# A transformer block with a routed expert layer on one core: the second norm of the first two sequences placed elsewhere in the order of the steps

## The chip, the cores and the metric

The kernel runs on 1 core of one Trainium2 chip. The metric is the device time of one execution in microseconds (us). Profiles are of one execution each.

## What is computed

Four sequences (b = 0 to 3) of 1024 tokens, width 256, pass through one block:

```python
mod = silu(c) @ wmod                     # sa, ca, ga, sb, cb, gb, per sequence
h = layernorm(x) * (1 + ca) + sa
x = x + ga * attention(h)                # 16 heads of width 16, causal
h = layernorm(x) * (1 + cb) + sb         # "the second norm"
logits = h @ gate_w                      # 8 experts, the best 2 with softmax weights
x = x + gb * sum_of_two_experts(h)       # per expert: silu(h @ w1) @ w2
```

## The kernel before

The kernel is written by hand for five engines: PE (matmuls), ACT (exps, copies, scaling), DVE (maxima, statistics, small arithmetic), POOL (element-wise work on pairs of tiles, and some transfers) and SP (the queue that issues most transfers). Each engine runs its own instructions strictly in order; semaphores tie them together.

`schedule()` writes one list, `order`, of steps. Each engine's program walks through the whole list and issues its own share of every step, so a step's place in the list sets its place on all five engines at once. A wait inside a step holds back everything that stands behind it on that engine, transfers on SP and POOL included.

**The attention** is sixteen groups, four heads each, four groups to a sequence: sequence b is in groups 4b to 4b + 3. This text counts groups from 0, as the code does, so the sixth, seventh, eighth and ninth group are groups 5, 6, 7 and 8. A group has 24 slots. In slot k of group w PE makes two score tiles (`score`, L1738, for the masked ones also L1742, into `PS`), ACT takes their exps (L1091, `PR<-PS`), PE multiplies the exps by V (`pv`, L1758). The other half of a slot belongs to a later group: two tiles for the row maxima (`max`, L1715 on PE into `PM`, L1425 and L1428 on DVE), 34 slots ahead (`LEAD`). So the maxima of group w + 2 begin in slot 14 of group w. There are three `PM` banks and three `PS` banks, so PE is held when DVE or ACT fall behind by more than that.

`place(w, k, parts)` puts a chain of steps into group w at slot k; each part has a delay in slots from the part ahead of it. Around the groups these chains run, and the change touches or meets them:

- `rep(g)`, group g - 2, slot 2, on SP: 12 transfers `QK<-SD` (L724) and a small one `QK<-ZR` (L758) that bring group g's split queries and keys on chip. PE's first `max` of group g waits for all of them. Every second group `sd` is ahead of it (slot 23 of an odd group, six stores `SD<-SP`, L737).
- `od(g - 1)`, group g, slot 4, on POOL: five small transfers (L708 `OP<-OS`, L709 `LD<-OS`) of a group's results and row sums.
- `lsum`, `recip`, `lrec`, `lrep` for a pair of groups, in groups 2, 4, 6, ... from slot 7: SP reads the row sums back (`LP<-LD`, L806), DVE takes their reciprocal at slot 11 (L1460, it waits for that transfer), SP writes them out (L809) and reads them spread (L814, `LP<-LR`); POOL's `div` at slot 17 (L954) uses them. `out(b)`, group 4b + 4 from slot 20, makes the attention's output on PE (L1770) and adds it on POOL (L960, L965).
- The second norm of sequence b: `x2` (SP stores x, L818), `stat2` (DVE, 8 tiles, bn_stats and bn_aggr, L1336 and L1338), `rstd` (16 small dependent DVE instructions on 128x8, L1364 to L1383, a root by Newton steps; the code calls turn 2 for this norm), `h2` (four pairs of tiles: two ACT instructions each, L1119, then two POOL instructions, L984 and L987), `h2st` (SP waits for all four `h2` and stores h, L823, `H2D<-XA`, 1 MB).
- The router's logits of sequence b, four times `lgt` (PE transposes, L1779; ACT copies, L1124), `lg` (PE, L1787; DVE copies, L1469), `top` (DVE, L1476 and L1478).

For b = 0 and 1 the helper `ln2(b)` is one chain from slot 10 of group 4b + 7: store and eight statistics, one per slot, sixteen root steps at half slots, `h2` three slots later and one per slot, then `h2st`; it runs into slots 5 to 9 of group 4b + 8, where the logits stand at slots 9, 11, 13 and 15.

After the groups come the routed experts (L1625 on PE) and the sum of the outputs; the change moves nothing there.

Of the kernel before, what the change touches and what calls it, by code (L numbers as in the profile page):

```python
# [16 lines left out]
NT = T // 128  # L17
# [91 lines left out]
def schedule():  # L109
# [10 lines left out]
    def place(w, k, parts):  # L120
        at.setdefault(NW * w + k, []).append(parts)
# [18 lines left out]
    def ln2(b, wait=3, pace=1, rest=0.5, n4=4):  # L140
        parts, d = [(0, ("x2", b))], 0
        for n in range(NT):
            parts.append((d, ("stat2", b, n)))
            d = 1 if n % pace == pace - 1 else 0
        parts += [(d if n == 0 else rest if n % (n4 if pace > 1 else 1) == 0 else 0, ("rstd", 2, b, n, 2)) for n in range(16)]
        return parts + [(1 if tp else wait, ("h2", b, tp)) for tp in range(4)] + [(1, ("h2st", b))]
# [4 lines left out]
    def logits(b, tp, rest=0.5):  # L151
        return [(0, ("lgt", b, tp)), (1, ("lg", b, tp)), (rest, ("top", b, tp, 0)), (rest, ("top", b, tp, 1))]
# [16 lines left out]
    def one(*step):  # L169
        return [(0, step)]  # L170
# [35 lines left out]
        for tp, k in enumerate((20, 22, 23, 25)):  # L206
            place(4 * b + 4, k, one("out", b, tp))
    for b in range(B - 2):
        place(4 * b + 7, 10, ln2(b))
        for tp in range(4):  # L210
            place(4 * b + 8, 9 + 2 * tp, logits(b, tp))
    place(NG - 3, 4, ln2(B - 2, 2, 2))
    for tp in range(4):
        place(NG - 3, 16 + 2 * tp, logits(B - 2, tp))
# [230 lines left out]
def adaln_block(nc, x, wqkvT, b_qk, b_v, woT, b_o, gate_w, w1, w2, cT, wmod, iota, out):  # L445
# [8 lines left out]
    with ctx:  # L454
# [140 lines left out]
        LR = nc.dram_tensor("LR", [2 * B, 8, T], F32).ap()  # L595

        order = schedule()
        names = dict.fromkeys(n for by in (FIRST, *SIGNALS.values()) for n in by)
        S = {n: Signal(ctx.enter_context(nc.semaphore(f"s_{n}"))) for n in names}
# [1308 lines left out]
```

## Time and profile before

| | us |
|---|---|
| median of 3 runs | 981.04 (980.57 to 982.25) |
| the profiled execution | 978.13 |
| its span in the profile | 976.4 |
| PE busy in the span | 881.6 (90%) |
| DVE busy | 704.4 (72%) |
| ACT busy | 579.8 (59%) |
| POOL busy | 387.5 (40%) |
| granted PE clock, mean | 0.983 |

The span is the time from the first to the last profiled instruction; some 1.7 us of the execution lie outside it. Busy time is the time in which an engine executes; a matmul's end is modelled, so a busy PE need not be at its peak. The profile's clock column is the share of the full 2.4 GHz that PE was granted.

### The profile page before, as it was taken

Reading aid. Unit: us, or ns where it says so; the run is one execution under the profiler, and the core shown is the slowest. Engines: PE = TensorE matmul, PEld = TensorE weight load, DVE = VectorE, ACT = ScalarE, POOL = GpSimd, SP = SyncE. Lnnn points to the kernel's source line nnn. Section 1 sums busy time; section 2 is a strip of 40 time slices with the busy share of each in tenths; the row PEclk is TensorE's granted clock in tenths of the full one; section 3 lists DMA queues with packets and bytes.
Section 4 is the critical chain, followed back from the end, with each engine's and each line's share of the span. In section 5 each row is a group of like instructions: output and inputs, shape, how many; then the busy total and the mean of one; then the engine's idle time right before and its main releaser. Section 6 shows DMA issues by size and latency. Waiting matters only on the chain.

```text
span 976.4 us, 19311 instructions
## 1 busy us (share of the span) xinstructions
PE 881.6 (90%) x6091; PEld 527.3 (54%) x6164; DVE 704.4 (72%) x2285; ACT 579.8 (59%) x1268; POOL 387.5 (40%) x386
## 2 busy tenths in 40 slices
PE   7898899998999998999999987878899999999990
PEld 3453444433535434544443443432799899999980
DVE  7887777879566889657689667899547575444588
ACT  3365477676676777586676757767535433333563
POOL 4213101731531435333143554124586465555630
PEclk8999999999999999999999999999999999999995
DMA  5487436525506437244364663206332323222699
GB/s 204 125 177 173 61 87 99 83 82 89 80 2 145 76 72 161 67 64 107 64 123 103 131 129 131 74 26 180 111 97 77 98 77 103 77 77 75 207 297 317
DMA packets 83596, 110.62 MB, mean 113 GB/s; under 512 B 16290, under 2 KB 56794, under 8 KB 83498
## 3 DMA queue, kind: packets, MB, share of 16 engines
q1 hardware_dynamic: 73194, 84.22, 36.3%
q0 software_dynamic: 9216, 22.80, 9.1%
q10 hardware_dynamic: 1088, 2.36, 0.7%
q8 instruction: 53, 0.87, 0.4%
q14 instruction: 45, 0.37, 0.1%
HBM read 69.42 MB, written 35.41 MB: 107 GB/s over the span
## 4 chain that ended last, share of the span: by engine, by line
PE 59%; DVE 11%; ACT 5%; DMA 4%; issue 4%; POOL 1%; SPq 1%; DVEq 0%; ACTq 0%; POOLq 0%
PE PY L1625 10%; PE PH L1625 10%; PE PO L1758 9%; PE PS L1738 8%; PE PM L1715 6%; PE PHT L1843 3%; ACT PR L1091 3%; PE PX L1770 3%; DVE MXF L1428 2%; DMA LD<-OS 2%; DVE JK L1425 2%; PE PX L1694 2%; PE PX L1690 2%; PE PS L1742 2%; PE PX L1679 1%
## 5 line engine op out<-in xcount | busy, mean ns | idle before, releaser
L1091 ACT ACTIVATE PR<-PS 128x512 f32<-128x512 f32 (+3 forms) x768 | 334.5, 498 | 126.5 <-PE PS L1742 92.6
L1425 DVE CUSTOM_DVE_ANT_0 JK<-PM,MK 128x128 bf16<-128x128 f32 (+3 forms) x512 | 238.4, 483 | 51.2 <-PE PM L1715 48.4
L1715 PE MATMUL PM<-QK 128*128 128x512 bf16 (+3 forms) x725 | 230.5, 326 | 27.0 <-DVE MXF L1428 12.7
L1738 PE MATMUL PS<-QK 128*128 128x512 bf16 (+3 forms) x738 | 233.4, 328 | 11.4 <-ACT PR L1091 9.1
L1428 DVE TENSOR_REDUCE MXF<-PM 128x1 f32<-128x512 f32 x256 | 175.0, 684 | 78.0 <-PE PM L1715 61.4
L1738 PEld LDWEIGHTS PS<-QK 128*128 128x128 bf16 x768 | 75.0, 98 | 165.9 <-ACT PR L1091 106.4
L1758 PE MATMUL PO<-PR,V 128*17 128x512 f32 (+3 forms) x1536 | 161.0, 491 | 0.0
L1715 PEld LDWEIGHTS PM<-QK 128*128 128x128 bf16 x768 | 75.0, 98 | 99.9 <-DVE MXF L1428 33.4
L1625 PE MATMUL PY<-W2S,HT 128*128 x852 | 119.3, 289 | 2.7 <-issue 1.8
L1742 PE MATMUL PS<-MT,identb 128*128 128x128 bf16 x512 | 111.4, 220 | 2.7 <-DMA QK<-CD 1.4
L1625 PE MATMUL PH<-W1S,XT 128*128 x426 | 111.7, 397 | 0.6 <-DVE W2S L1580 0.6
L1154 ACT ACTIVATE HS<-PH 128x512 f32<-128x512 f32 x71 | 42.4, 597 | 114.6 <-PE PH L1625 114.6
L1625 PEld LDWEIGHTS PY<-W2S,HT 128*128 128x128 f32 x852 | 106.4, 190 | 3.2 <-issue 3.2
L1015 POOL DMA_INDIRECT YT<-YO,ROW x71 | 75.4, 1062 | 75.3 <-DVE YO L1600 43.5
L1588 DVE TENSOR_TENSOR XT<-PXT,XT 128x256 fp32r<-128x256 f32 x71 | 29.9, 422 | 98.0 <-ACT XT L1148 97.7
L1009 POOL DMA_INDIRECT XL<-H2D,TOK x71 | 78.4, 1105 | 46.2 <-PE PXT L1822 20.6
L1625 PEld LDWEIGHTS PH<-W1S,XT 128*128 128x128 f32 x426 | 75.7, 189 | 13.4 <-issue 0.8
L932 POOL TENSOR_TENSOR SF<-SF,SP 128x512 f32<-128x512 f32 x28 | 32.6, 1163 | 126.0 <-ACT SP L1081 124.7
L708 POOL DMA_DIRECT2D OP<-OS x60 | 29.7, 501 | 112.8 <-ACT OS L1098 112.4
L1742 PEld LDWEIGHTS PS<-MT,identb 128*128 128x128 bf16 x512 | 50.4, 98 | 29.8 <-issue 3.2
L954 POOL TENSOR_TENSOR OP<-OP,LP 128x1024 f32<-128x1024 f32 x7 | 16.5, 2355 | 100.9 <-DMA LP<-LR 78.6
L1593 DVE TENSOR_TENSOR HT<-PHT,HT 128x512 fp32r<-128x512 f32 x71 | 49.0, 690 | 3.9 <-ACT HT L1162 0.2
(284 smaller groups left out, 1199.4 us busy)
## 6 DMA issues: line engine op xcount, KB each, us to landing
QK<-SD SPq DMA_DIRECT2D x180, 128.0 KB
SD<-SP SPq DMA_DIRECT2D x42, 256.0 KB, 3.0
LP<-LR SPq DMA_DIRECT2D x64, 64.0 KB
W1S<-in_w SPq DMA_DIRECT2D x8, 512.0 KB, 7.2
OP<-OS POOLq DMA_DIRECT2D x60, 64.0 KB, 6.5
X<-XA SPq DMA_DIRECT2D x3, 1024.0 KB, 11.8
H2D<-XA SPq DMA_DIRECT2D x3, 1024.0 KB, 4.5
YG<-YT SPq DMA_DIRECT2D x12, 256.0 KB, 5.0
```

The lines of the kernel that those rows point to most:

```text
L1009: eng.indirect_dma_start(XL[:, t % 3, :], None, H2D[0:(B if t >= NA else B - 1) * T, :], bass.IndirectOffsetOnAxis(ap=TOK[:, t:t + 1], axi ...
L1015: eng.indirect_dma_start(YT, bass.IndirectOffsetOnAxis(ap=ROW[:, t:t + 1], axis=0), YO[:, t % 4, :], None, bounds_check=EMPTY - 1 + B * T ...
L1091: eng.activation(PR[:, slot, i, c0:512], PS[m % 3][:, c0:512], ACT.Exp, scale=0.25).then_inc(S["exp"].sem, 1)
L1154: eng.activation(HS[:, t % 2, :], PH[t % 2][:, :], ACT.Silu).then_inc(S["silu"].sem, 1)
L1425: eng.tensor_tensor_reduce(JK[:, jk % 2, 0:w], PM[m % 3][:, 0:w], MK[:, 512 - w:512], 1.0, -3.0e38, ALU.add, ALU.max, MXA[:, mb, h, qt:qt ...
L1428: eng.tensor_reduce(MXF[:, mb, h, qt - 4:qt - 3], PM[m % 3][:, 0:w], AX.X, ALU.max).then_inc(S["mx"].sem, 1)
L1593: eng.tensor_tensor(HT[:, t % 2, 1, :, :], PHT[t % 2][:, :, :], HT[:, t % 2, 0, :, :].bitcast(F32), ALU.subtract).then_inc(S["hlo"].sem, 1)
L1625: last = eng.matmul(out_, stat[:, part, c, :], wt[:, bass.ds(v, 1), c, :].rearrange("p a n -> p (a n)"), start=(j == 0 and c == 0), stop=( ...
L1715: eng.matmul(PM[m % 3][:, 0:128 * (k1 - k0)], QK[:, r, h, 0, qt * 128:(qt + 1) * 128], QK[:, r, h, 1, k0 * 128:k1 * 128], start=True, stop ...
L1738: last = eng.matmul(PS[m % 3][:, c0:512], QK[:, r, h, 1, j * 128:(j + 1) * 128], QK[:, r, h, 0, 512 * f + c0:512 * f + 512], start=True, s ...
L1742: last = eng.matmul(PS[m % 3][:, c0:c0 + 128], identb[:, :], MT[:, :], start=False, stop=True, skip_group_check=True)
L1758: last = eng.matmul(PO[32 * i:32 * i + 17, c0:512], V[g // 4 % 2][:, j, 4 * (g % 4) + i, :], PR[:, (m - 1 + i // 2) % SLOTS, i % 2, c0:512 ...
```

## The change

The four steps of the second norm of sequences 0 and 1 are taken apart and placed one by one. `x2` and `stat2` go to slots 6 to 13 of group 4b + 5 (groups 5 and 9), the root steps to group 4b + 6 from slot 4 (groups 6 and 10), the scaling `h2` to slots 19 to 22 of group 4b + 7 (groups 7 and 11), `h2st` to slot 0 of group 4b + 8 (groups 8 and 12). The logits of sequence 0 go from group 8 to group 10; those of sequence 1 stay in group 12. The instructions themselves are the same.

```diff
     for b in range(B - 2):
-        place(4 * b + 7, 10, ln2(b))
+        place(4 * b + 5, 6, [(0, ("x2", b))] + [(1, ("stat2", b, n)) for n in range(NT)])
+        place(4 * b + 6, 4, [(0.5 if n else 0, ("rstd", 2, b, n, 2)) for n in range(16)])
         for tp in range(4):
-            place(4 * b + 8, 9 + 2 * tp, logits(b, tp))
+            place(4 * b + 7, 19 + tp, one("h2", b, tp))
+            place((10, 12)[b], 9 + 2 * tp, logits(b, tp))
+        place(4 * b + 8, 0, one("h2st", b))
```

The changed file is three lines longer, so each line number behind this place is 3 higher in it (L823 is L826, L984 is L987, L1460 is L1463).

SP's queue from the end of group 7 into group 8, before (`SD<-SP` is `sd` of pair 5, `QK<-ZR` and `QK<-SD` are `rep(10)`, `LP` are the row sums of groups 6 and 7, `H2D<-XA` is `h2st`):

```order
70 L737 DMA SD<-SP 128x1024 x6
71 L758 DMA QK<-ZR 3x4x1024
72 L724 DMA QK<-SD 16x4x1024 x12
73 L806 DMA LP<-LD 128x64
74 L823 DMA H2D<-XA 128x8x256
75 L809 DMA LR<-LP 128x64
76 L814 DMA LP<-LR 16x1024 x8
```

and in the changed kernel:

```order
70 L740 DMA SD<-SP 128x1024 x6
71 L826 DMA H2D<-XA 128x8x256
72 L761 DMA QK<-ZR 3x4x1024
73 L727 DMA QK<-SD 16x4x1024 x12
74 L809 DMA LP<-LD 128x64
75 L812 DMA LR<-LP 128x64
76 L817 DMA LP<-LR 16x1024 x8
```

The store of h has moved from behind the row sums to ahead of the 12 copies of `rep(10)`. The same stands at group 12, where `rep(14)` and one weight load come behind it.

POOL at the same place, before (`SF` and `SP` are `qk_hi` and `qk_lo` of pair 5, `OP<-OS` and `LD<-OS` are `od(7)`, `XA<-XA,G` is `h2`):

```order
86 L932 TENSOR_TENSOR SF<-SF,SP 128x512
87 L938 TENSOR_TENSOR SP<-SF,SP 128x512
88 L708 DMA OP<-OS 16x1024 x4
89 L709 DMA LD<-OS 4x1024
90 L984 TENSOR_TENSOR XA<-XA,G 128x512
91 L987 TENSOR_TENSOR XA<-XA,G 128x512
```

and in the changed kernel:

```order
86 L935 TENSOR_TENSOR SF<-SF,SP 128x512
87 L987 TENSOR_TENSOR XA<-XA,G 128x512
88 L990 TENSOR_TENSOR XA<-XA,G 128x512
89 L941 TENSOR_TENSOR SP<-SF,SP 128x512
90 L987 TENSOR_TENSOR XA<-XA,G 128x512
91 L990 TENSOR_TENSOR XA<-XA,G 128x512
92 L987 TENSOR_TENSOR XA<-XA,G 128x512
93 L990 TENSOR_TENSOR XA<-XA,G 128x512
94 L987 TENSOR_TENSOR XA<-XA,G 128x512
95 L990 TENSOR_TENSOR XA<-XA,G 128x512
96 L711 DMA OP<-OS 16x1024 x4
97 L712 DMA LD<-OS 4x1024
```

The eight instructions of `h2` (four pairs) have moved from behind `od(7)` to ahead of it, the first pair also ahead of the last subtraction of `qk_lo`.

## Rows read from the trace of the kernel before

**Rows 1.** Busy us (count) PE, PEld, DVE, ACT, POOL; clock, DMA, GB/s: groups 4, 8, 10, 12
```profile
216.00:254.70 38.70, 34.85 (x248) 15.88 (x250) 32.21 (x123) 23.33 (x53) 9.93 (x10) 1.00 0.46 86
...
369.90:413.80 43.90, 40.29 (x294) 21.72 (x298) 34.99 (x158) 28.64 (x65) 20.11 (x18) 1.00 0.47 90
...
455.80:491.70 35.90, 35.31 (x254) 17.38 (x257) 24.92 (x89) 23.69 (x54) 9.02 (x10) 1.00 0.49 89
...
529.30:571.50 42.20, 40.20 (x295) 21.56 (x299) 28.31 (x127) 28.50 (x66) 20.08 (x18) 1.00 0.56 121
```
**Rows 2.** POOL, groups 7 and 8: start, us, instruction, [idle before <- releaser]
```profile
364.34 1.16 POOL L932 TENSOR_TENSOR SF<-SF,SP 128x512 f32<-128x512 f32 x1
366.22 1.15 POOL L938 TENSOR_TENSOR SP<-SF,SP 128x512 bf16<-128x512 f32 x1 [0.72 <-DVE SP L1401]
374.20 1.96 POOL L708 DMA_DIRECT2D OP<-OS  x4 [6.82 <-ACT OS L1098]
376.15 0.58 POOL L709 DMA_DIRECT2D LD<-OS  x1
377.48 1.26 POOL L984 TENSOR_TENSOR XA<-XA,G 128x512 f32<-128x512 f32 x1 [0.76 <-ACT XA L1119]
...
387.10 1.27 POOL L987 TENSOR_TENSOR XA<-XA,G 128x512 f32<-128x512 f32 x1
399.33 2.35 POOL L954 TENSOR_TENSOR OP<-OP,LP 128x1024 f32<-128x1024 f32 x1 [10.96 <-DVE CP L1449]
```
**Rows 3.** Groups of instructions by line: ACT's half of the scaling
```profile
L1119 ACT ACTIVATE XA<-XA,RT,RS 128x256 f32<-128x256 f32 x24 | 13.1, 600 | 0.0
```
**Rows 4.** SP's issues in order of time, group 8
```profile
370.31 5.58 SPq L724 DMA_DIRECT2D QK<-SD  x12
385.72 0.34 SPq L806 DMA_DIRECT2D LP<-LD  x1
388.47 0.38 SPq L823 DMA_DIRECT2D H2D<-XA  x1
388.90 0.57 SPq L809 DMA_DIRECT2D LR<-LP  x1
393.74 3.57 SPq L814 DMA_DIRECT2D LP<-LR  x8
```
**Rows 5.** Windows of 2 us in group 8, the columns of rows 1
```profile
374.00:376.00 2.00, 2.00 (x17) 0.77 (x17) 2.00 (x8) 1.23 (x4) 1.80 (x4) 1.00 1.12 142
...
384.00:386.00 2.00, 1.84 (x20) 1.42 (x21) 1.67 (x7) 1.39 (x4) 1.78 (x3) 1.00 0.05 9
...
390.00:392.00 2.00, 1.91 (x15) 1.30 (x13) 2.00 (x14) 2.00 (x5) 0.00 (x0) 1.00 1.03 346
```
**Rows 6.** PE in group 8: the first matmul for the maxima of group 10
```profile
390.88 0.22 PE L1715 MATMUL PM<-QK 128*128 128x128 bf16 x1
```
**Rows 7.** DVE in order of time: the reciprocal in groups 4 and 12
```profile
232.76 0.52 DVE L1460 RECIPROCAL LP<-LP 128x64 f32<-128x64 f32 x1
...
548.15 0.55 DVE L1460 RECIPROCAL LP<-LP 128x64 f32<-128x64 f32 x1 [1.55 <-DMA LP<-LD]
```
**Rows 8.** SP's issues in group 12, and the landing of its weight load (last column)
```profile
536.50 0.41 SPq L839 DMA_DIRECT2D W1S<-in_w  x1
545.23 0.34 SPq L806 DMA_DIRECT2D LP<-LD  x1
...
W1S<-in_w SPq DMA_DIRECT2D x1, 512.0 KB, 10.6
```
**Rows 9.** PE and its clock after an early stall: timeline, then windows of 2 us
```profile
46.85 0.22 PE L1722 MATMUL PX<-identb,CPH 128*48 128x128 bf16 x1 [2.15 <-DVE CPH L1449]
...
48.00:50.00 2.00, 1.78 (x6) 0.55 (x5) 2.00 (x7) 0.00 (x0) 1.15 (x1) 0.55 0.03 6
50.00:52.00 2.00, 2.00 (x6) 0.70 (x5) 1.20 (x3) 0.00 (x0) 0.00 (x0) 0.60 0.45 119
```
**Rows 10.** DVE in order of time: a root step of 8 columns in group 8
```profile
399.53 2.17 DVE L1377 TENSOR_TENSOR RT<-RS 128x8 f32<-128x8 f32 x1
```

## The prediction

> **What bounds the kernel now.** I read the busy table of the page first: PE executes in 90% of the span, DVE in 72%. Then the windows by group, whose borders are the first of each group's 48 exps in ACT's timeline. Group 8 lasts 43.9 us with 40.3 of PE, group 12 42.2 with 40.2, group 10 35.9 with 35.3 [rows 1]. So a group costs its PE work plus 0.6 to 3.6 us in which PE stands, and the change can win only out of that, since it removes no instruction. Group 4 (38.7 us, 34.9 of PE) is what group 8 is without logits and scaling: it has the same output steps and the same statistics of a later sequence's first norm. Last, the timelines of POOL and SP, because the change moves work past other work there, and in-order queues make others wait for it.
>
> **What moves and costs nothing.** The eight statistics (groups 5, 9) and sixteen root steps (groups 6, 10) go into groups where DVE has room: in group 10 it is busy 24.9 of 35.9 us [rows 1]. ACT's part of the scaling is eight instructions of 0.60 us [rows 3]; it now stands between the short exps, and POOL needs twice as long for its part, so ACT is no pacer. The store of x goes to group 5, where nobody waits for it. For all four groups together I take +0.6 us (bounds 0 and 2).
>
> **The scaling on POOL.** It now stands behind the fourth subtraction of group 7, which ends at 364.34 + 1.16 = 365.5. The eight instructions took 377.48 to 388.37, or 10.9 us, and one subtraction (1.15, with gaps 1.3) goes in between [rows 2]. So the chain ends at 365.5 + 0.1 + 10.9 + 1.3 = 377.8. Before, POOL was free until 374.20, when it issued the five transfers of group 7's results [rows 2]; these now start 3.6 us later and end about 380.4.
>
> **The store of h on SP.** `h2st` waits for all four pairs, and behind it stand the 12 copies of `rep(10)`. Before, their first was issued at 370.31 [rows 4]; now the store goes at 377.9 and the first copy, behind it and the small copy of zeros, near 379.1: 8.8 us later. The transfers themselves: the store's 1.05 MB moved at 346 GB/s and was through about 4.4 us after its issue at 388.47, since SP's next issue that needed it gone is at 393.74 [rows 4, 5], so it ends at 382.3. The copies with the five transfers beside them are 1.57 + 0.28 MB at 142 GB/s, 13.0 us; before, they were through just after 384 [rows 5]. Now they end at 382.3 + 13.0 = 395.3. PE asked for them at 390.88 [rows 6], and would ask at about 388 with logits and waits gone from the slots ahead. The slack before was 6 us, the delay is 11.
>
> **The row sums.** `LP<-LD` was issued 9.0 us after the last of the five transfers (376.7 to 385.72) [rows 2, 4], so now at about 389.5. But it goes into the same queue as the copies. A small transfer behind a large one lands behind it: `LR<-LP`, 32 KB, was issued at 388.90 right behind the store, and SP could not go on to what needs it before 393.74 [rows 4], just after the store was through. The page "DMA: Bandwidth & Descriptors" of the Trainium skill (Queues, rings and completion order) says that a ring's descriptors are consumed in order; by that rule, the trace agrees, `LP<-LD` waits for the copies; it speaks against this change, and the sum with it is the one below, without it that of rival 1. In group 12 of before the reciprocal came 1.0 us behind the landing of the large load ahead of its row sums (547.1 and 548.15) [rows 7, 8]. So now it starts at 395.3 + 1.0 = 396.3. DVE would reach it 16.8 us after the group's first exp (232.76 - 216.00, group 4) [rows 1, 7], that is near 385 to 387, and behind it stand all later maxima, for which PE waits after three banks. **Both PE's copies and DVE's row sums are late by about 10 us.** From the reciprocal to the next group's first exp it was 254.70 - 232.76 = 21.9 us in group 4 [rows 1, 7]. So group 9 starts at 418.2, against 413.8: **+4.4 us** for group 8, its lost logits already in it.
>
> **Group 12.** POOL's and SP's work repeats 159.5 us later (`LP<-LD` at 545.23 and 385.72) [rows 4, 8]. The chain ends at 537.3, the store is through at 541.8, the copies at 554.8. Behind them is a weight load of 0.52 MB [rows 8], half the store, 1.5 us: 556.3. The reciprocal starts 1.0 later, at 557.3. Before, it started at 548.15, already after 1.55 us of waiting for that transfer [rows 7], which had the weight load (landing 536.50 + 10.6 = 547.1) ahead of it [rows 8]. The logits stay here, so the rest of the group is as it was: **+9.2 us**.
>
> **Logits in group 10.** Group 8 has 40.29 - 34.85 = 5.4 us more PE work than group 4 [rows 1], and I charge them in group 10, with 0.8 us of waits for the shared bank (group 12 stands 2.0 us, group 10 0.6; part of that is scaling): **+6.2** (bounds 5.4 and 7.5).
>
> **The clock.** The groups of before have no stall of PE as long as these. The nearest row: after one of 2.15 us at 46.85, the granted clock was 0.55 and 0.60 in two windows of 2 us [rows 9], so about half, 1.2 of 2.4 GHz, for most of 4 us. While PE is the bound, this costs about 1.7 us. Bounds per stall 0 (the clock holds, or DVE paces) and 3.4 (twice as long); I take 1.7, twice: **+3.4**.
>
> **Sum.** 4.4 + 9.2 + 6.2 + 3.4 + 0.6 = 23.8 us on the profiled 978.13, or 1001.9. The median of the runs is 2.9 above that execution, 981.04, so I forecast 1004.8 for the median after. The gains the change has are in this: the roots beside POOL's work and DVE's full slots in groups 7, 8, 11 and 12 go, but they lie ahead of or inside a stall that a chain on POOL and SP sets, and are swallowed by it.
>
> **Rival 1: only the copies hold.** If `LP<-LD` slips past the copies, it lands near 391.5, and PE is held by its first maximum alone. From that matmul group 8 took 413.8 - 390.9 = 22.9 us, less 2.7 for the two of four logits that follow it: 20.2, so group 9 starts at 415.5, +1.7. In group 12 the same matmul stands at about 529.3 + 21.0 = 550.3 and goes at 554.8: +4.5. With 6.2 + 0.6 and one share of the clock, 1.7, this is +14.7: 995.7. For it: the five transfers use another queue and do get through between the copies. Against: `LP<-LD` doesn't use that queue, and the row of `LR<-LP`. Chance 0.2.
>
> **Rival 2: faster.** The chain on POOL ends early enough, or the copies overtake the store, and nothing is held. Then the waits in the crowded groups go. A root step on 8 columns took 2.17 us [rows 10] beside POOL's product of 2.35 us from 399.33 [rows 2], and the roots of this norm leave such places. The most to win is PE's standing time in groups 8 and 12, 3.6 + 2.0 [rows 1], with 0.8 given back in group 10: 976.2. The page "SBUF — State Buffer" of the Trainium skill (SBUF: two separate sides) has the rule behind it: a DVE instruction with two operands in SBUF and one of GpSimd lock each other out for a whole instruction; by that rule the trace agrees, and the rule is for this change. It decides at the copies: they must be through by about 388, so the store must be gone before 371. The eight instructions at 1.27 us behind 365.5 forbid that; it would need them much shorter or an earlier start, and the order gives neither. Chance 0.07, and 0.03 for gains and stalls that cancel within 0.2% (about what a measurement of this kernel can tell from no change).
>
> **Rival 3: slower still.** Store, copies and POOL's five transfers share the engines worse than in sequence, and the row sums' later legs (`LR`, `LP<-LR`, `div`, `out`) are late too, 3 to 4 us a group, or the clock stays low for twice the time: 1009 to 1015. Chance 0.12. The forecast itself has 0.58.
>
> **Numbers.** The range takes in rival 1 down to its sum without clock and with the lower logits (981 + 1.7 + 4.5 + 5.4 is 992.6, less 1.6 for waits that the statistics' move may end), 991, and part of rival 3, 1012. Faster 0.07, same 0.03, slower 0.90.
>
> **What would show it.** In the trace after: POOL's eight scaling instructions solid from 365.5 to about 378; `H2D<-XA` issued at 378 and `QK<-SD` behind it; DVE idle some 10 us ahead of the reciprocal in group 8 with `LP<-LD` as releaser, 9 in group 12; PE standing as long, and a clock below 1 behind it; group 9 starting 4.4 us later than before, group 10 near 42 us with little standing. I am wrong if the first copy of `rep(10)` goes before 375, if the reciprocal finds its row sums there, or if group 12 is no longer than before.

## The result, and the profile after

| | before | after |
|---|---|---|
| median of the runs, us | 981.38 (980.57 to 982.25, 4 runs) | 1004.46 (1000.04 to 1005.51, 4 runs) |
| ratio, 95% interval | | 1.0231 (1.0209 to 1.0253) |
| the profiled execution, us | 978.13 | 1005.01 |
| its span, us | 976.4 | 1003.3 |
| PE, DVE, ACT, POOL busy, us | 881.6, 704.4, 579.8, 387.5 | 899.3, 700.9, 580.2, 387.6 |
| granted PE clock, mean | 0.983 | 0.963 |

The change costs 23.1 us, 2.3%; the forecast was 1004.8. The two profiled executions lie 26.9 us apart in their spans, because the one of before is faster than its median. The same work is done, so the time lies in stands and in the clock. The windows by group of the changed kernel (columns as in [rows 1]: PE, PEld, DVE, ACT, POOL busy, the granted clock, DMA share, GB/s), for groups 4, 7, 8, 10, 12, 13 and 14:

```profile
214.00:252.50 38.50, 35.09 (x251) 15.95 (x250) 31.91 (x123) 23.20 (x53) 9.93 (x10) 1.00 0.45 86
330.20:366.70 36.50, 35.69 (x242) 14.74 (x240) 26.99 (x92) 28.98 (x66) 15.20 (x17) 1.00 0.45 81
366.70:417.70 51.00, 37.18 (x251) 16.10 (x251) 32.40 (x124) 23.65 (x55) 18.41 (x17) 0.90 0.38 85
459.30:501.00 41.70, 41.39 (x306) 23.16 (x305) 28.36 (x133) 25.99 (x58) 8.97 (x10) 1.00 0.41 78
537.60:593.70 56.10, 44.19 (x300) 23.87 (x300) 28.17 (x120) 25.46 (x59) 18.37 (x17) 0.85 0.39 86
...
593.70:640.40 46.70, 39.92 (x281) 18.37 (x280) 35.12 (x141) 32.11 (x69) 17.73 (x17) 0.93 0.61 160
640.40:679.90 39.50, 31.37 (x283) 13.27 (x281) 34.47 (x118) 24.58 (x56) 6.29 (x10) 0.96 0.13 29
```

Against [rows 1], group 8 went from 43.9 to 51.0 us although it lost the logits, group 12 from 42.2 to 56.1, group 10 from 35.9 to 41.7. In groups 8 and 12 PE is busy 13.8 and 11.9 us less than the window lasts, and the clock is below 1. In group 10 nothing waits: 41.39 of 41.70 is PE work. Groups 7 and 11 are 1.0 us shorter each (36.6 for 37.6 from exp to exp), as the statistics and root steps beside them are gone.

The cause in group 8 is read on three queues. POOL in order of time, against [rows 2]:

```profile
363.49 1.44 POOL L987 TENSOR_TENSOR XA<-XA,G 128x512 f32<-128x512 f32 x1
...
366.43 1.16 POOL L941 TENSOR_TENSOR SP<-SF,SP 128x512 bf16<-128x512 f32 x1
...
374.90 1.27 POOL L990 TENSOR_TENSOR XA<-XA,G 128x512 f32<-128x512 f32 x1
376.11 1.98 POOL L711 DMA_DIRECT2D OP<-OS  x4
403.47 2.35 POOL L957 TENSOR_TENSOR OP<-OP,LP 128x1024 f32<-128x1024 f32 x1 [24.82 <-issue]
```

SP's issues, against [rows 4]:

```profile
376.27 0.37 SPq L826 DMA_DIRECT2D H2D<-XA  x1
...
377.49 9.57 SPq L727 DMA_DIRECT2D QK<-SD  x12
387.17 0.35 SPq L809 DMA_DIRECT2D LP<-LD  x1
394.65 0.34 SPq L812 DMA_DIRECT2D LR<-LP  x1
```

DVE at the stand, in order of time:

```profile
394.07 0.55 DVE L1463 RECIPROCAL LP<-LP 128x64 f32<-128x64 f32 x1 [10.53 <-DMA LP<-LD]
```

and PE:

```profile
395.23 0.61 PE L1718 MATMUL PM<-QK 128*128 128x512 bf16 x1 [10.45 <-DVE MXF L1431]
```

The store of h is issued in the moment in which POOL's last scaling instruction ends (374.90 + 1.27 = 376.17). Behind it the 12 copies need 9.57 us to be issued (5.58 before), the read of the row sums lands 6.9 us after its issue, DVE stands 10.5 us on it, and PE, its three banks full, 10.4 us on DVE. The windows through this stand:

```profile
388.00:390.00 2.00, 0.00 (x0) 0.00 (x0) 0.00 (x0) 0.00 (x0) 0.00 (x0) 0.82 1.06 153
390.00:392.00 2.00, 0.00 (x0) 0.00 (x0) 0.00 (x0) 0.00 (x0) 0.00 (x0) 0.50 1.00 132
392.00:394.00 2.00, 0.00 (x0) 0.00 (x0) 0.00 (x0) 0.00 (x0) 0.00 (x0) 0.50 0.13 23
...
396.00:398.00 2.00, 2.00 (x12) 0.41 (x10) 1.93 (x12) 1.13 (x2) 0.00 (x0) 0.50 0.26 66
```

The DMA engines are full (1.06, 1.00) while every compute engine stands, and idle from 393. The clock falls to half, 1.2 GHz, while PE stands, and is still there when PE works again. Group 12 is the same, later and with the weight load between (SP's issues):

```profile
546.84 0.37 SPq L826 DMA_DIRECT2D H2D<-XA  x1
...
548.06 10.13 SPq L727 DMA_DIRECT2D QK<-SD  x12
558.30 0.40 SPq L842 DMA_DIRECT2D W1S<-in_w  x1
558.80 0.40 SPq L809 DMA_DIRECT2D LP<-LD  x1
```

DVE, and PE behind it:

```profile
566.79 0.55 DVE L1463 RECIPROCAL LP<-LP 128x64 f32<-128x64 f32 x1 [13.53 <-DMA LP<-LD]
...
567.95 0.61 PE L1718 MATMUL PM<-QK 128*128 128x512 bf16 x1 [11.73 <-DVE MXF L1431]
```

The clock is at half from 389.3 to 399.5 in group 8 and from 559.9 to 577.0 in group 12. A good part of both stretches lies in the stand itself, where no matmul runs: behind the end of the stand PE works at half clock for 4.3 us (395.2 to 399.5) in group 8 and for 9.1 us (567.95 to 577.0) in group 12.

### The profile page after: what moved, and what is told of

Its sections match the earlier page's. It is cut to its first block, busy times and chain, and to the rows that moved or that the text cites. A ratio compares the mean times of both kernels' runs of the same rounds, so it can differ in the third digit from the quotient of the medians.

```text
span 1003.3 us, 19384 instructions
## 1 busy us (share of the span) xinstructions
PE 899.3 (90%) x6164; PEld 532.5 (53%) x6164; DVE 700.9 (70%) x2285; ACT 580.2 (58%) x1268; POOL 387.6 (39%) x386
## 4 chain that ended last, share of the span: by engine, by line
PE 68%; DVE 13%; ACT 5%; POOL 5%; issue 4%; DMA 3%; SPq 3%; DVEq 0%; POOLq 0%; ACTq 0%
PE PO L1761 10%; PE PH L1628 10%; PE PY L1628 10%; PE PS L1741 9%; PE PM L1718 8%; PE PHT L1846 3%; PE PX L1773 2%; PE PX L1693 2%; DVE MXF L1431 2%; PE PX L1697 2%; PE PX L1682 2%; ACT PR L1094 2%; SPq L727 2%; PE PS L1745 2%; DVE JK L1428 2%
## 5 line engine op out<-in xcount | busy, mean ns | idle before, releaser
L1718 PE MATMUL PM<-QK 128*128 128x512 bf16 (+3 forms) x768 | 247.4, 331 | 42.8 <-DVE MXF L1431 34.9
L1741 PE MATMUL PS<-QK 128*128 128x512 bf16 (+3 forms) x768 | 247.6, 334 | 9.1 <-ACT PR L1094 7.8
L1761 PE MATMUL PO<-PR,V 128*17 128x512 f32 (+3 forms) x1536 | 164.7, 501 | 0.0
L1628 PE MATMUL PH<-W1S,XT 128*128 x426 | 114.4, 405 | 0.6 <-DVE W2S L1583 0.6
L1018 POOL DMA_INDIRECT YT<-YO,ROW x71 | 75.3, 1061 | 76.0 <-DVE YO L1603 44.2
L1628 PEld LDWEIGHTS PH<-W1S,XT 128*128 128x128 f32 x426 | 77.5, 194 | 13.9 <-issue 0.9
L1745 PEld LDWEIGHTS PS<-MT,identb 128*128 128x128 bf16 x512 | 50.4, 98 | 29.2 <-issue 2.3
```

The lines of the kernel that those rows point to most:

```text
L1018: eng.indirect_dma_start(YT, bass.IndirectOffsetOnAxis(ap=ROW[:, t:t + 1], axis=0), YO[:, t % 4, :], None, bounds_check=EMPTY - 1 + B * T ...
L1628: last = eng.matmul(out_, stat[:, part, c, :], wt[:, bass.ds(v, 1), c, :].rearrange("p a n -> p (a n)"), start=(j == 0 and c == 0), stop=( ...
L1718: eng.matmul(PM[m % 3][:, 0:128 * (k1 - k0)], QK[:, r, h, 0, qt * 128:(qt + 1) * 128], QK[:, r, h, 1, k0 * 128:k1 * 128], start=True, stop ...
L1741: last = eng.matmul(PS[m % 3][:, c0:512], QK[:, r, h, 1, j * 128:(j + 1) * 128], QK[:, r, h, 0, 512 * f + c0:512 * f + 512], start=True, s ...
L1745: last = eng.matmul(PS[m % 3][:, c0:c0 + 128], identb[:, :], MT[:, :], start=False, stop=True, skip_group_check=True)
L1761: last = eng.matmul(PO[32 * i:32 * i + 17, c0:512], V[g // 4 % 2][:, j, 4 * (g % 4) + i, :], PR[:, (m - 1 + i // 2) % SLOTS, i % 2, c0:512 ...
```

## The experiments

**1. Which part of the change makes the stands.** Points 1 to 4 have four kernels, measured together with the kernel before (980.29 us). Each ratio below is to the kernel before measured at the same time, whose median moved between 980.3 and 982.0 us from one set to the next. First the changed kernel with only the store moved:

```diff
-        place(4 * b + 8, 0, one("h2st", b))
+        place(4 * b + 8, 9, one("h2st", b))
```

> The changed kernel with one edit: the store of h (and its wait) stands at slot 9 of groups 8 and 12, behind the copies and the read of the row sums, as before the change. Theory A (the store's place ahead of the copies makes the stall, on SP): the copies are issued near 368 in group 8, 9 us earlier than in the changed kernel; the row sums are still some us late, because POOL issues their transfers behind the scaling, so the reciprocal waits 3 to 5 us where it waited 10.5 and 13.5; time 985 to 993. Theory B (the scaling's place on POOL, ahead of the five transfers of the row sums, makes the stall): the reciprocal still waits 9 us or more, time 1000 to 1005.

Measured 986.31 us (983.27 to 989.27), ratio 1.006 (1.0036 to 1.0084): 6.0 us above before are left of 23.1, so 17.1 are gone. Its issues on SP in group 8:

```profile
369.31 6.76 SPq L727 DMA_DIRECT2D QK<-SD  x12
383.23 0.34 SPq L809 DMA_DIRECT2D LP<-LD  x1
```

and its reciprocals on DVE in groups 8 and 12:

```profile
385.13 0.55 DVE L1463 RECIPROCAL LP<-LP 128x64 f32<-128x64 f32 x1 [1.10 <-DMA LP<-LD]
...
547.84 0.55 DVE L1463 RECIPROCAL LP<-LP 128x64 f32<-128x64 f32 x1 [5.34 <-DMA LP<-LD]
```

The copies go at once, and `LP<-LD` lands 1.9 us after its issue (6.9 behind the copies). So the place of the store on SP is the main cause. What is left shows in group 12, which takes 48.1 us for 42.1: the reciprocal waits 5.3 us, PE stands 3.5 us, and the clock is at half from 548.2 to 558.4. POOL's scaling has a part in this, since it puts the five transfers 9.1 us behind the group's first exp (4.3 before), but a small one: in the first kernel of experiment 8 POOL issues them at 4.2 us, and group 12 is 47.0 us all the same, with 3.8 us of waiting and as long at half clock. Most of what is left comes because DVE, with no scaling in the slots ahead, reaches the reciprocal before the row sums.

**2. The wait or the megabyte.** A store ahead of the copies does two things: SP waits for the scaling, and 1 MB moves first. Here SP only waits, and the store is at slot 9:

```diff
-        place(4 * b + 8, 0, one("h2st", b))
+        place(4 * b + 8, 0, one("h2w", b))
+        place(4 * b + 8, 9, one("h2st", b))
...
+                elif kind == "h2w":
+                    for tp in range(4):
+                        sp.wait_ge(*after("h2", "h2", a[0], tp))
```

> The changed kernel with the store of h at slot 9 of groups 8 and 12, but with its wait for the scaling left at slot 0 ahead of the copies, so SP is held as in the changed kernel and no megabyte stands ahead of the copies. If the hold of SP and the megabyte add, as the forecast had them (8.8 us and 3 to 4.4 us), each group gains 3 to 4 us on the changed kernel: 996 to 999. If the megabyte alone is the trouble, the time is that of the kernel with the store late; if the hold alone is, it stays within 2 us of 1004.5.

Measured 999.9 us (996.94 to 1000.2), ratio 1.0188 (1.0155 to 1.022). Above before are left 19.6 us here, 23.1 in the changed kernel and 6.0 in the first experiment: 13.6 come with the wait alone, 3.5 with the megabyte. The second figure is little more than the noise of four runs each; the profiles have 13.3 and 6.0 for the same two steps, in the lengths of groups 8 and 12 (51.0 and 56.1, 49.0 and 52.1, 39.7 and 48.1). The time lies 0.9 above the expected 996 to 999. Its issues on SP in group 8 (its lines are numbered 2 higher still):

```profile
377.06 0.75 SPq L763 DMA_DIRECT2D QK<-ZR  x1
377.86 6.59 SPq L729 DMA_DIRECT2D QK<-SD  x12
```

Without the store ahead, the 12 issues take 6.59 us for 9.57: the slow issue was mostly the store's doing, the late start the wait's.

**3. The logits back in group 8**, all else as changed:

```diff
-            place((10, 12)[b], 9 + 2 * tp, logits(b, tp))
+            place(4 * b + 8, 9 + 2 * tp, logits(b, tp))
```

> The changed kernel with the logits of the first sequence back in group 8. Theory A: group 10 loses 5.7 us; in group 8 the part of them ahead of the reciprocal falls into the stall and costs nothing, the rest costs about 3 us: 1001 to 1003. Rival (logits cost the same wherever they stand, the stall is not set by a fixed chain): within 1 us of 1004.5.

Measured 1006.37 us (1004.45 to 1007.18), ratio 1.0259 (1.0228 to 1.029): no gain. Its windows of groups 8 and 10:

```profile
366.10:423.30 57.20, 44.52 (x299) 23.64 (x299) 34.87 (x152) 25.72 (x58) 18.39 (x17) 0.88 0.36 76
465.20:501.20 36.00, 35.73 (x258) 17.37 (x257) 26.13 (x105) 23.73 (x54) 9.05 (x10) 1.00 0.51 90
```

Group 10 gives 5.7 us back and group 8 takes 6.2. Both expected ranges missed (1001 to 1003, and within 1 us of 1004.5). The theory had hidden logits under the stand: DVE's reciprocal is in slot 11, so half of the logits come behind the stand. Of the 6.2 us, 5.3 lie behind the reciprocal, and the clock stays at half to 404.2 there (399.5 in the changed kernel).

**4. The scaling and the store back too**, only the statistics (groups 5, 9) and roots (6, 10) moved:

```diff
-            place(4 * b + 7, 19 + tp, one("h2", b, tp))
-            place((10, 12)[b], 9 + 2 * tp, logits(b, tp))
-        place(4 * b + 8, 0, one("h2st", b))
+            place(4 * b + 8, 5 + tp, one("h2", b, tp))
+            place(4 * b + 8, 9 + 2 * tp, logits(b, tp))
+        place(4 * b + 8, 9, one("h2st", b))
```

> Of the change only the statistics in groups 5 and 9 and the roots in groups 6 and 10 are kept; scaling (slots 5 to 8), store (slot 9) and logits (from slot 9) stand in groups 8 and 12 as before the change. Theory A: the early parts are harmless and end 1 us of waits in groups 7 and 11 each, with up to 1 us more in group 8: 977.5 to 980. Rival (early statistics and roots cost what they save, DVE being full elsewhere): within 1 us of 981.4.

Measured 978.41 us (975.3 to 983.26), ratio 0.9985 (0.9962 to 1.0007). Measured again, together with the kernels of experiments 5 and 6 and the first of experiment 8:

> The run with only statistics in groups 5 and 9 and roots in groups 6 and 10 once more, as it was, beside the two above: 977 to 979.5 if its first result (978.4 for 980.3) was no chance; 980 to 981.5 if it was.

Measured 979.28 us (974.28 to 985.63), ratio 0.9996 (0.9973 to 1.002). Both medians are 1 to 2 us below before and both intervals hold 1: this part of the change does no harm; that it gains is not shown by the times. Groups 7 and 11 are 36.5 us (37.6 before) in both profiles, but group 8 is 46.9 and 45.3 us (43.9 before), with one or two stretches of 3.4 us at half clock that the profile of before doesn't have there; why they come is open.

**5. The logits alone in group 10**, on top of the kernel of point 4:

```diff
-            place(4 * b + 8, 9 + 2 * tp, logits(b, tp))
+            place((10, 12)[b], 9 + 2 * tp, logits(b, tp))
```

> Only statistics in groups 5 and 9, roots in 6 and 10 and the logits of sequence 0 in group 10; scaling and store of h where they were. Compare with the run that has the logits in group 8 and is otherwise the same (978.4 before, and again in this job). Theory: the logits cost PE time wherever they stand, about 5.5 us; group 10 grows by 5.7 as in the changed kernel (to 41.7) and group 8 falls by as much less what it stood anyway: within 1.5 us of the other run either way. Rival, they were under a wait of group 8 that stays: group 8 falls by 3 us or less and the time is 980.5 to 982.

Measured 981.96 us (979.75 to 987.88), ratio 1.0021 (1.0001 to 1.0041), 2.7 us above the same kernel with the logits in group 8, measured beside it (979.28). The two intervals overlap, so the times alone don't settle it. The profiles bear the rival out: group 10 pays its 5.7 us in full (41.7), and group 8 gives back 0.8 (44.5 for 45.3). Without the logits PE comes to the output steps sooner and stands there until POOL's division is done:

```profile
400.54 2.04 PE L1773 MATMUL PX<-WO,OP 128*128 128x256 f32 x4 [3.77 <-POOL OP L957]
```

The clock is at half from 399.0 to 405.8, so part of what the logits gave back went into this stand and the clock behind it.

**6. The clock.** The changed kernel, with 40 matmuls in group 8 whose result nobody reads, ahead of the place where PE stood; they change no output:

```diff
+     place(8, 12, one("busy"))
...
+                elif kind == "busy":
+                    pe.wait_ge(*after("ct", "crow", 8, 2))
+                    for n in range(40):
+                        eng.matmul(PX[:, :], identb[:, :], MK[:, :], start=True, stop=True)
```

> The changed kernel, and in group 8 PE runs 40 matmuls of 128x512 bf16 more (identity times mask, into a bank that nobody reads then), a little ahead of the place where it stood 10.4 us. They add nothing to the output; each is some 0.22 us, 8.7 us together. Theory clock: the clock falls because PE stands, so with the stand filled it stays at 1.0 behind it, the way from the reciprocal to group 9's first exp is 21.8 to 22.2 us again (changed kernel 23.6), group 8 is 1.5 to 2 us shorter (49.0 to 49.5 for 51.0), and the time 1002.4 to 1003.2. Rival, the low clock costs nothing because DVE paces there: 23.4 to 23.8 us, time 1004.5. Third way, the added work outlasts the stand or delays what DVE waits for: the gap ahead of the reciprocal or behind it grows and the time is 1006 or more.

Measured 1005.48 us (1003.7 to 1005.79), ratio 1.0249 (1.0226 to 1.0272). (Its lines are numbered 2 higher still up to the steps of PE, those there 6.) PE at the place:

```profile
385.37 8.80 PE L1704 MATMUL PX<-MK,identb 128*128 128x512 bf16 x40
...
398.08 0.39 PE L1724 MATMUL PM<-QK 128*128 128x512 bf16 x1 [2.18 <-DVE MXF L1433]
```

DVE's reciprocal there:

```profile
396.93 0.55 DVE L1465 RECIPROCAL LP<-LP 128x64 f32<-128x64 f32 x1 [10.90 <-DMA LP<-LD]
```

And windows of 2 us around the end of the stand:

```profile
396.00:398.00 2.00, 0.00 (x0) 0.00 (x0) 1.07 (x3) 0.59 (x2) 0.00 (x0) 1.00 0.01 1
398.00:400.00 2.00, 1.74 (x13) 0.47 (x13) 2.00 (x11) 1.09 (x2) 0.00 (x0) 1.00 0.12 33
```

The clock stays at 1.00. DVE waits as long as ever, and from the reciprocal to group 9's first exp (419.1) it is 22.1 us, against 23.6 in the changed kernel: the low clock cost 1.5 us in group 8. Group 12, where nothing was added, kept its half clock (560.5 to 577.6). Group 8 is 49.9 us, above the expected 49.0 to 49.5, since the reciprocal came 0.4 us later into it. The whole time does not show the gain: 1.5 us is below what four runs can tell.

**7. Do the copies alone hold PE?** The changed kernel, and the reciprocal in groups 8 and 12 behind the maxima of slot 14, so that DVE's wait can't hold PE there (`("recip", u)` 7.5 slots behind `lsum` for u = 3 and 5, in place of 4; the two legs behind it 0.5 slot each):

> The changed kernel with the reciprocal of the row sums in groups 8 and 12 3.5 slots later (slot 14.5, behind the maxima of slot 14), all else as changed. PE's order is the same, and its first maximum of group 10 (slot 14) waits for the 12 copies. Rival 1's view, that the reciprocal made the stand and the copies alone hold less: PE works on through slots 11 to 13, reaches slot 14 near 388 and goes on when the copies are through, at 393; from there some 20 us and the clock's share to group 9: group 8 is 46 to 48 us (51.0 in the changed kernel), group 12 48 to 52 (56.1), time 993 to 998. The forecast's view, both are late by about 10 us and either alone holds as long: group 8 50 to 51, group 12 54 to 56, time 1001 to 1005.

Measured 1007.97 us (1004.53 to 1009.16), ratio 1.0255 (1.021 to 1.03). PE's long waits in group 8:

```profile
398.91 0.29 PE L1718 MATMUL PM<-QK 128*128 128x128 bf16 x1 [9.62 <-DMA QK<-SD]
414.44 0.77 PE L1773 MATMUL PX<-WO,OP 128*128 128x256 f32 x1 [5.10 <-POOL OP L957]
```

and POOL's division there:

```profile
412.01 2.33 POOL L957 TENSOR_TENSOR OP<-OP,LP 128x1024 f32<-128x1024 f32 x1 [29.29 <-DMA LP<-LR]
```

PE now stands 9.6 us in group 8 with `QK<-SD` as releaser, and 9.0 in group 12. So the copies alone hold it nearly as long as the row sums did. That refutes rival 1's price for the copies (+1.7 us in group 8); its other half, that `LP<-LD` slips past them, the changed kernel's trace had refuted already. The time is above both expected ranges, because the later reciprocal makes the division late and PE stands 5.1 us more at the output of group 8, with another 6.8 us at half clock behind it: group 8 takes 55.9 us, while group 12, where PE stands only 1.0 us on the division, takes 54.1, within the forecast's 54 to 56.

**8. A version without the collisions.** The statistics and roots as changed, the logits back, the scaling in slots 12, 15, 18, 21 of group 4b + 6 and the store in slot 5 of group 4b + 7:

```diff
-            place(4 * b + 7, 19 + tp, one("h2", b, tp))
-            place((10, 12)[b], 9 + 2 * tp, logits(b, tp))
-        place(4 * b + 8, 0, one("h2st", b))
+            place(4 * b + 6, 12 + 3 * tp, one("h2", b, tp))
+            place(4 * b + 8, 9 + 2 * tp, logits(b, tp))
+        place(4 * b + 7, 5, one("h2st", b))
```

> The changed kernel with the scaling in group 4b + 6 (slots 12, 15, 18, 21), the store of h in slot 5 of group 4b + 7, and the logits of sequence 0 back in group 8. Theory: the loss came only from POOL's eight instructions ahead of the five transfers and from the store ahead of the 12 copies; both are gone here, and what the freed slots of groups 7, 8, 11 and 12 are worth shows alone: groups 7 and 11 1 us shorter, groups 8 and 12 shorter by up to their standing time less logits' share, 1 to 3 us each, group 6 and 10 longer by 0 to 1: 974 to 979. Rival: scaling and store cost the same wherever they stand, or a new wait comes up in group 6 or 10 (OUT's work on POOL): 981 or more.

Measured 981.47 us (977.01 to 986.39), ratio 1.0008 (0.9991 to 1.0026): the rival's number. Groups 6 and 10, which have the scaling now, took 37.5 us (36.0 before), and group 12 took 47.0. Its reciprocal there, on DVE:

```profile
547.45 0.55 DVE L1463 RECIPROCAL LP<-LP 128x64 f32<-128x64 f32 x1 [3.84 <-DMA LP<-LD]
```

PE's wait behind it:

```profile
548.61 0.55 PE L1718 MATMUL PM<-QK 128*128 128x512 bf16 x1 [2.04 <-DVE MXF L1431]
```

and a window of 2 us some 5 us later:

```profile
554.00:556.00 2.00, 2.00 (x9) 0.49 (x5) 0.25 (x1) 0.57 (x1) 0.00 (x0) 0.50 0.01 4
```

With the scaling gone from slots 5 to 8, DVE comes to the reciprocal 15.6 us into the group (17.3 before) and the row sums land at 19.5 (18.8 before). PE stands only 2.0 us, but the clock is low behind it, from 548.7 to 558.9 in the trace's clock records. So the reciprocal alone was put 1.5 slots later in groups 8 and 12:

```diff
-            ... (4, ("recip", u)), (1, ("lrec", u)), (2, ("lrep", u))])
+            ... (5.5 if u in (3, 5) else 4, ("recip", u)), (0.5 if u in (3, 5) else 1, ("lrec", u)), (1 if u in (3, 5) else 2, ("lrep", u))])
```

> The run with the scaling in groups 6 and 10, and in groups 8 and 12 DVE's reciprocal of the row sums 1.5 slots later (slot 12.5). There the reciprocal waited 3.8 us in group 12, PE stood 2.0 us, and the granted clock was at half for 10.2 us behind it; group 12 took 47.0 us. Theory: the wait is short of work ahead, not a slow transfer, and the low clock follows PE's stand; 1.5 slots (3 to 4 us) later the wait is under 1 us, PE stands under 0.5, no half-clock stretch of more than 3.4 us follows, group 12 is 41 to 42.5 us, and the time is 976 to 979. Rival: div or the output steps of group 12 become late by as much (POOL waits for LP<-LR) and group 12 is 44 or more; or the low clock is there without a stand of PE: 980 to 982.

Measured 977.65 us (976.07 to 982.48), ratio 0.9965 (0.9941 to 0.9989). The window of group 12 of this kernel:

```profile
528.30:568.40 40.10, 39.86 (x299) 21.91 (x298) 27.78 (x119) 25.20 (x57) 9.95 (x10) 1.00 0.46 96
```

and its reciprocal on DVE:

```profile
547.48 0.54 DVE L1463 RECIPROCAL LP<-LP 128x64 f32<-128x64 f32 x1
```

DVE no longer waits there, the clock is 1.00, and the group is 40.1 us for 47.0: with the clock behind it, a wait of DVE of 3.8 us had cost 6.9 in the profiled execution. The medians, each against before measured beside it, differ by 3.8 us (0.9 above and 2.8 below).

The last two ask where the scaling stands best; the reciprocal stays at slot 12.5 in both. With two pairs in slots 5 and 7 and two in slots 15 and 16 of group 4b + 7, the store in slot 19:

> As the run beside it, with the scaling not in group 4b + 6 but in slots 5, 7, 15 and 16 of group 4b + 7, where POOL has idle stretches of 8 and 6 us, and the store of h in slot 19 there, ahead of the stores of sd. Theory: groups 6 and 10 are 36.0 us again (37.5 with the scaling in them) and groups 7 and 11 stay at 36.5 to 37, since neither POOL nor ACT is needed there: 1.5 to 3 us less than the run beside it, 974 to 977. Rival: the store meets the stores of sd and rep, or ACT's eight instructions hold up the exps: groups 7 and 11 are 38 or more, or the reciprocal of group 8 waits again: 979 or more.

Measured 982.63 us (979.58 to 987.89), ratio 1.0024 (0.9998 to 1.005), again the rival's number. Groups 6 and 10 are 36.0 us as expected, but groups 7 and 11 are 39.9. POOL in group 7, in order of time:

```profile
360.71 1.27 POOL L990 TENSOR_TENSOR XA<-XA,G 128x512 f32<-128x512 f32 x1
362.16 1.15 POOL L935 TENSOR_TENSOR SF<-SF,SP 128x512 f32<-128x512 f32 x1 [0.17 <-POOL XA L990]
```

and PE, its longest wait there:

```profile
364.55 0.28 PE L1718 MATMUL PM<-QK 128*128 128x256 bf16 x1 [2.54 <-DVE MXF L1431]
```

The later pairs hold up POOL's subtraction of `qk_hi`, which stands ahead of PE in a chain over DVE. With one pair in slot 12 of group 4b + 6 and three in slots 5, 6.5 and 8 of group 4b + 7, the store in slot 12 there:

> As the run with the reciprocal at slot 12.5 (977.7 for 980.5 of before), and the scaling's four pairs in slot 12 of group 4b + 6 and slots 5, 6.5 and 8 of group 4b + 7, all in POOL's idle stretch of 8 us there, the store of h in slot 12. Theory: POOL's subtractions of qk_hi at 344.85 are not held up as they were with two pairs in slots 15 and 16 (groups 7 and 11 were 39.9), so groups 7 and 11 are 36.5 to 37.2, groups 6 and 10 36.3 to 36.6 (37.5 with four pairs): 974.5 to 977. Rival: ACT's instructions among the exps of slots 5 to 8 cost as much as in groups 6 and 10: 977 to 979.

Measured 977.31 us (972.12 to 981.73), ratio 0.9955 (0.993 to 0.9979), 0.3 us above the theory's range. The groups are as the theory had them; the windows of its groups 6 and 7:

```profile
294.70:331.20 36.50, 35.81 (x258) 17.23 (x257) 26.16 (x105) 24.67 (x57) 11.63 (x12) 1.00 0.49 87
331.20:367.70 36.50, 35.70 (x243) 14.82 (x242) 27.02 (x92) 28.34 (x65) 21.01 (x21) 1.00 0.49 109
```

and of groups 8 and 12:

```profile
367.70:410.80 43.10, 40.43 (x300) 21.70 (x299) 34.38 (x152) 25.53 (x58) 9.97 (x10) 1.00 0.41 77
525.70:565.80 40.10, 39.86 (x299) 21.90 (x298) 27.84 (x119) 25.20 (x57) 9.96 (x10) 1.00 0.52 96
```

Both this kernel and the one at 977.65 are faster than before, by 0.45% and 0.35%, small steps whose intervals leave 1 out; between the two the runs don't decide.

## Why the prediction was right, step by step

In lengths of groups in the two profiles, with its clock terms put where they belong:

| | predicted | measured |
|---|---|---|
| group 8 | +4.4 + 1.7 | +7.0 |
| group 10 | +6.2 | +5.7 |
| group 12 | +9.2 + 1.7 | +13.9 |
| groups 5, 6, 7, 9, 11 | +0.6 | -2.3 |
| ahead of group 4; from group 13 on | 0 | -2.0; +4.7 |

The first four rows give 23.8 predicted and 24.3 measured, so the total is right partly because misses of both signs cancel. That the forecast of the median came within 0.3 us is luck on top: between the profiles the difference is 26.9 us, between the medians 23.1.

- **The scaling on POOL** was right in kind and 1.6 us short. The chain ended 9.5 us after group 8's first exp (376.17 - 366.7) where the forecast had 7.9 (377.8 - 369.9). The subtraction ahead of it ended 3.4 us ahead of that exp (4.4 before), and within the chain the first instruction was longer (1.44) and the last pair waited 0.44.
- **The store on SP** was right: issued as the chain ended, copies behind it. From its issue to the reciprocal it took 17.8 us in group 8 and 19.9 in group 12, where the forecast had 18.4 and 19.9. It left out that the 12 issues stretch behind a store, 9.57 us for 5.58, but that did not set the end. Two misses cancel in it: the store landed 5.8 us after its issue (4.4 forecast), and the copies needed some 11 us behind it (13.0 forecast). Experiment 2 splits the loss into 13.6 us of waiting and some 3.5 to 6 of megabyte.
- **The row sums** behave as the forecast had it: `LP<-LD` lands 6.9 us after its issue behind the copies and 1.9 us after it when they are through (experiment 1). The page "DMA: Bandwidth & Descriptors" of the Trainium skill (Queues, rings and completion order) has descriptors of a ring consumed in order, though it promises no order of completion; by the order of consumption a small read waits behind the copies, and the trace agrees with its 6.9 us for 1.9. The reciprocal came 27.4 us into group 8, against 17.8 before: +9.6, with 8.6 predicted. Experiment 7 shows that the copies hold PE for 9.6 us by themselves, so both halves of the forecast's sentence, copies and row sums late by about 10 us, are shown.
- **Group 12** was mis-sized most, by 3.0 us. The reciprocal came 29.2 us into the group for 18.8 (+10.4; predicted 9.2), and from there to group 13 it took 26.9 us for 23.3 (+3.6; predicted 1.7). The second is the clock term: behind the stand the clock stays at half for 9.1 us, over logits and maxima, and PE's busy time in the group is 44.2 us for 40.2. The forecast had taken the stretch of [rows 9] there, most of 4 us; this term was mis-sized, and 3.6 is just above its own upper bound of 3.4, the clause of rival 3 that the clock stays low for twice the time. The first is POOL's chain once more: the store is issued 9.25 us into the group where the forecast had 8.1.
- **The clock in group 8** was right: 4.3 us at half behind the stand, 23.6 us from the reciprocal to group 9, and 22.1 with PE kept busy in the same place, so 1.5 for the 1.7 taken.
- **Logits in group 10** were right (5.7 for 6.2). That they are worth less than that in group 8 is experiment 5: 5.7 us more in a group without waits, and 0.8 back in the profiles, 3 by the medians.
- **Statistics and roots** were taken at +0.6 in groups 5, 6, 9 and 10, which show nothing of it, and gave 2.3 us back in groups 7, 9 and 11. Part of this gain is the one that rival 2 names: in group 7 of before two root steps took 0.78 and 0.99 us at 364.75 and 366.41 and ended with POOL's subtractions of 364.34 and 366.22 [rows 2], where a step takes 0.15 to 0.17 otherwise; in the changed kernel no root step of this norm takes over 0.4. The statistics left group 7 too, so the two shares aren't separated. The sentence that these gains are swallowed was wrong for groups 7 and 11, which end before the stand; experiment 4 has the same 1 us in each.
- **Rival 2**, faster, named the right gain and an obstacle that is real, but not the only one: with store and scaling out of the way the time is still 981.47, and only with the reciprocal later as well 977.65, against rival 2's 976.2.
- **Outside the places of the change**, +4.7 us from group 13 on and -2.0 ahead of group 4 were in no term. From group 13 on the clock falls several times for a few us, without a long stand of PE; here in a window of the changed kernel, behind a stand of 1.4 us at 607:

```profile
608.00:610.00 2.00, 2.00 (x9) 0.60 (x6) 1.83 (x11) 1.08 (x2) 0.00 (x0) 0.50 0.96 342
```

The profile of before had none there, but in the clock records of all twelve profiles of the experiments there are one to five of them between 580 and 725 us, those of the fastest kernels included. So nothing ties them to the change alone; whether the changed kernel has more of them than the kernel before has in other executions is open.

## What to carry to other kernels

A step that is moved earlier takes its waits along: before moving a store up an in-order queue, look at what stands behind it there and at which moment its own input is ready, since here the wait cost at least twice what the bytes did. Where two late transfers hold an engine one after the other (here the copies PE itself, the row sums PE by way of DVE), relieving one shows nothing until the other is relieved too. And an engine that gets faster reaches its next wait sooner: where a group has been cleared, move the waiting instruction back by as much as was won, or the new wait, and the clock behind it, eats the gain.

## What was not expected of the hardware

- 12 issues of copies by SP took 5.6 to 7.6 us in groups 8 and 12 of all kernels in which the 1 MB store of h did not stand ahead of them (6.59 with the same late start), and 9.5 to 10.8 in those in which it did (9.57 and 10.13 in the changed kernel): the queue holds back the issuer, not only the data.
- A stand of PE of 2.0 us was followed by 10.2 us at half clock in the kernel of 981.47 us (window 554:556 at 0.50 with PE busy 2.00), with PE at work in all of it; behind the stand of 10.4 us in the changed kernel PE worked at half clock for 4.3 us only. In experiment 6 a stand of 2.2 us right behind dense matmuls left the clock at 1.00. So the length of the stand alone doesn't decide it, and what does isn't settled here.
